# Dividing each pair's pooled rows by its sums of weights inside a copy, with chunks 1 to 3 reordered and short matmuls ahead of the program

## The chip, the cores and the metric

The kernel runs on one core of one Trainium2 chip. The metric is the device time of one execution in microseconds, as the median of 3 runs. One execution was also profiled, with every instruction and every DMA packet in time.

## The reference

Attention pooling of a recommendation model: 512 users, 200 behaviours each, 128 features.

```
h = relu(behavior @ W_b + (candidate @ W_c)[:, None, :] + fc1_b)      # 512 x 200 x 128
scores = h @ fc2_w + fc2_b                                            # 512 x 200
attn = softmax(scores, axis=-1)
user_interest = einsum('bse,bs->be', behavior, attn)                  # 512 x 128
x = concatenate([user_interest, candidate], axis=1)                   # 512 x 256
z = relu(x @ mlp1_w + mlp1_b)                                         # 512 x 256
logit = z @ mlp2_w + mlp2_b                                           # 512
```

All inputs are float32. The behaviours are 52 MB and are read twice, once as they are (`x`) and once transposed (`xt`).

## The kernel before

**Tiling.** A chunk is 16 users; there are 32 chunks, 0 to 31. A chunk's transposed data are four groups g0 to g3 of 800 columns. PE multiplies each group by `W_b` into one of three `z_ps` buffers of two banks; from chunk 2 on each group is six fp32r matmuls (L665, L666 and L669: high part by high weights, high part by low weights, low part by high weights), for which ACT makes the high part `xh` (L369) and DVE the low part `xl` (L500). A `z_ps` buffer is free again when its relu has been taken: g1 and g3 by ACT (L411, with the bias), g0 and g2 by DVE (L510, `biased_max`).

**Pairs.** Scores, softmax and pooling go by pairs of chunks. In the middle of each even chunk c from 4 on, after its group g1 (`PHASE_AT`), PE does: `transpose_sums` of an older pair (L733), `score` of chunks c-2 and c-1 (L682, 40 small fp32 matmuls), `weighted_sum` of chunks c-4 and c-3 into `u_ps` (L694, 56 small fp32 matmuls). Of fp32 matmuls every one leaves two load records and two matmul records in the trace, so the scores of a pair are 160 records, its weighted sums 224, and a group of six fp32r matmuls 12. DVE then takes the maxima of the scores (`softmax`, steps 0 to 6: step 0 is the transpose L521 and the last two make `exp_bias`, L540), ACT the exponentials with their row sums as an accumulated output (`exponents`, L376, `weight_sums`), and GpSimd spreads the weights by rows (`mask_weights`, L340). ACT copies the pooled sums of a pair from `u_ps` (`copy_pooled4`, L382), PE transposes them, ACT copies the result to `pooled_t` (L386).

**Start.** PE warms up with 9 matmuls of 128x128 by 128 (L799, unread output). Chunks 0 and 1 use plain fp32 products (L660). In `period`, phase 0, 1, 2 and 3 are chunks 0 to 3, and phase 4 is each later one but the last. In phase 1 and 3 ACT casts the first group of the next chunk before it takes the relu of g1. In phase 2 DVE does the whole softmax of chunks 0 and 1, and ACT their exponentials, before the last relu of chunk 2.

**Loops and queues.** `periods` writes chunks 0 to 3 out, and puts the rest in a loop over 4 chunks; PE's loop runs 7 times (chunks 4 to 31), and a straight tail follows. Each engine runs its list in order and waits on semaphores. All loads go through the queue that SP issues to, in a written order: per two chunks `xt` of c and c+1, then `x` of two older chunks, 1.6 MB each; SP waits for the buffer (four of each kind) before each.

**Tail.** The division by the sums of weights is done at the end in two parts (chunks 0 to 27, and 28 to 31). For each: `row_sums` (one matmul, L751), `inverses` on DVE (L549, L552), `spread_inverses` on PE (L757), `normalise` on DVE (L562), and then `mlp_pooled` (L776). The other operand of the MLP is `mlp_candidates` (L770), and `logits` (L783) ends each part. Chunks 30 and 31 have weighted sums of their own (`weighted_sum_alone`).

Of the kernel before, what the change touches and what calls it, by code (L numbers as in the profile page):

```python
# [11 lines left out]
P = 128  # L12
# [23 lines left out]
WARM_UP = 9  # L36
# [4 lines left out]
MASK_COLS = {"row_mask": 3 * ROWS, "fold": Q, "row_first": ROWS, "own_row": EACH, "same_row": P}  # L41
# [18 lines left out]
def attention_pooling_kernel(nc, behavior, behavior_t, cand_rest, weights_1, first, masks, later, out):  # L60
# [13 lines left out]
    with ExitStack() as ctx:  # L74
# [40 lines left out]
        row_mask, fold, row_first, own_row, same_row = (part_of(masks_sb, MASK_COLS, n) for n in MASK_COLS)  # L115
# [3 lines left out]
        pair_half = [slice(0, ROWS), slice(ROWS, 2 * ROWS)]  # L119
        row_mask = row_mask[:, ROWS:2 * ROWS]  # L120
# [11 lines left out]
        inv_sums = sb("inv_sums", [P, CHUNKS])  # L132

        inv_sel = xt[0][:, 0, 0:B].rearrange("p (c r) -> p c r", r=ROWS)
        pooled_n = xt[1][:, 0, 0:B]
# [14 lines left out]
        inverse_ps = [end_banks[0][1], end_banks[2][0]]  # L150
        mlp_ps = [end_banks[1], [s_ps[:, :], u_ps[:, :]]]
        logit_ps = [end_banks[2][1], inverse_ps[0]]
# [39 lines left out]
        mlp_step = [sem(f"mlp_step{i}") for i in range(2)]  # L192
        row_sums_done = sem("row_sums_done")
        inv_done = sem("inv_done")
# [158 lines left out]
        def _(act):  # L353
# [67 lines left out]
            def period(c, q, phase):  # L421
# [25 lines left out]
                biased_relu(c, q, 1, phase)  # L447
                for g in range(GROUPS):
                    next_half(g)

                for n in range(2):
                    exponents(c - 2 + n, n, pair_steps(c - 2) + 2 * (PAIR_STEPS - 1 + n), phase == 2)
                if phase > 2:
                    copy_pooled4(c - X_BUFS + 1, u_ps)
# [3 lines left out]
            copy_pooled_t(LAST - 4, u_ps[:, P:P + 2 * ROWS])  # L458
# [10 lines left out]
        def _(dve):  # L469
# [74 lines left out]
            def inverses(part, step):  # L544
                a, b = PART_CHUNKS[part]
                row_sums = inverse_ps[part]
                if step == 1:
                    dve.wait_ge(row_sums_done, part + 1)
                    op = nc.vector.reciprocal(inv_sums[:, a:b], row_sums[:, 0:b - a])  # L549
                if step == 2:  # L550
                    dve.wait_ge(mlp_step[part], 1)
                    op = nc.vector.tensor_tensor(  # L552
                        inv_sel[:, a:b, :], inv_sums[:, a:b].unsqueeze(2).to_broadcast([P, b - a, ROWS]),
                        row_first.unsqueeze(1).to_broadcast([P, b - a, ROWS]), ALU.mult)
                op.then_inc(mlp_step[part], 1)

            def normalise(part):
                a, b = PART_CHUNKS[part]
                inv = inverse_ps[part]
                dve.wait_ge(inv_done, part + 1)  # L560
                dve.wait_ge(pooled_t_copied, b + 2)
                nc.vector.tensor_tensor(pooled_n[:, a * ROWS:b * ROWS], inv[:, 0:(b - a) * ROWS],  # L562
                                        pooled_t[:, (a + 2) * ROWS:(b + 2) * ROWS], ALU.mult).then_inc(mlp_step[part], 1)
# [5 lines left out]
            def period(c, q, phase):  # L569
# [54 lines left out]
            inverses(0, 1)  # L624
            inverses(0, 2)
# [3 lines left out]
            normalise(0)  # L629
            inverses(1, 1)  # L630
            inverses(1, 2)
# [7 lines left out]
            normalise(1)  # L639
# [5 lines left out]
        def _(pe):  # L645
# [26 lines left out]
            def score(c, q, taken):  # L672
                pe.wait_ge(hidden_made, c * HALF + HALF)
                pe.wait_ge(relu_made, c * HALF + HALF)
                if taken is not None:

                    pe.wait_ge(softmax_step, taken)
# [30 lines left out]
            def weighted_sum(c, q):  # L708
                pe.wait_ge(x_loaded[q], loads(c, q))
                pe.wait_ge(masked, c + 1)  # L710
                if q % 2 == 0:

                    pe.wait_ge(pooled4_copied, c + 2)
                sum_tiles(c, q, u_ps, 0, WHOLE_TILES, GROUPS - 1).then_inc(pooled_done, 1)
# [31 lines left out]
            def row_sums(part):  # L746
                a, b = PART_CHUNKS[part]
                pe.wait_ge(weights_made, b)

                pe.wait_ge(relu_made, LAST * HALF + part + 1)  # L750
                nc.tensor.matmul(inverse_ps[part][:, 0:b - a], same_row, weight_sums[:, a:b],  # L751
                                 start=True, stop=True).then_inc(row_sums_done, 1)

            def spread_inverses(part):
# [152 lines left out]
```

## Time and profile before

| | |
|---|---|
| median of 3 runs | 267.79 us (267.74 to 267.81) |
| the profiled execution | 267.95 us |
| its span in the trace | 266.1 us (1.85 us lie around it) |
| PE busy | 254.9 us, 96% of the span |
| DVE, ACT, POOL busy | 205.4, 198.6, 28.9 us |
| DMA | 105.80 MB, busy to the ninth tenth or more in slices 2 to 37 of 40 |

Busy shares are means over stages. The chain that ended last is a path through the instructions, followed back from the last one. "Issue" is idle time of an engine for which no semaphore or transfer accounts in the profile. A row of the timeline is: start, length (us), engine, line, operation, output and inputs, count; in brackets the idle time before it and what ended it.

### The profile page before, as it was taken

The page shows a single profiled execution, that of the slowest core. Times are in us where ns is not written, and L with a number is a line of the kernel's source. Part 1 is how long each engine was busy: PE and PEld are TensorE (multiplying, and loading weights), DVE is VectorE, ACT ScalarE, POOL GpSimd, SP SyncE. Part 2 cuts the span into 40 slices and gives each one's busy share as a digit, 9 for nine tenths or more (in the row PEclk, how much of TensorE's full clock was granted, in tenths as well). Part 3 has the DMA queues.
Part 4 walks back from the last instruction along what each step waited for, and adds up shares of the span by engine and source line. Part 5 has one row for each costly group of instructions (what it writes and reads, how often), then busy time and mean ns, then how long its engine had stood idle before and what let it go on. Part 6 is the DMA issues. An engine that isn't in the chain of part 4 may idle for free.

```text
span 266.1 us, 10392 instructions
## 1 busy us (share of the span) xinstructions
PE 254.9 (96%) x3944; PEld 215.3 (81%) x3944; DVE 205.4 (77%) x316; ACT 198.6 (75%) x482; POOL 28.9 (11%) x39
## 2 busy tenths in 40 slices
PE   8989798979999999999999999999999999999795
PEld 7547587868888888888888888888888888888664
DVE  0458976977889796979798896979798997969221
ACT  2469685985969698896969696997887997957111
POOL 2000201102020110202020110202020201102100
PEclk9999799999999999999999999999999999999999
DMA  7999999999999999999999999999999999999700
GB/s 246 427 429 426 426 423 420 423 420 426 426 427 431 425 425 421 429 429 425 431 427 423 425 425 429 427 429 423 423 429 425 429 427 427 427 421 424 320 2 0
DMA packets 10684, 105.80 MB, mean 398 GB/s; under 512 B 1200, under 2 KB 1712, under 8 KB 2864
## 3 DMA queue, kind: packets, MB, share of 16 engines
q1 hardware_dynamic: 10384, 105.44, 94.3%
q10 hardware_dynamic: 288, 0.20, 0.2%
q8 instruction: 8, 0.13, 0.2%
q14 instruction: 4, 0.03, 0.0%
HBM read 105.63 MB, written 0.00 MB: 397 GB/s over the span
## 4 chain that ended last, share of the span: by engine, by line
PE 88%; DMA 4%; issue 3%; DVE 2%; SPq 1%; ACT 1%; DVEq 0%; ACTq 0%
PE z_ps L665 18%; PE s_ps L682 17%; PE z_ps L666 16%; PE z_ps L669 16%; PE u_ps L694 16%; DMA xt<-in_behavior_t 4%; PE z_ps L694 1%; PE z_ps L733 1%; PE z_ps L776 1%; SPq L263 1%; PE z_ps L770 1%; ACT hidden_rest L411 0%; DVE xl L500 0%; PE z_ps L757 0%; SPq L267 0%
## 5 line engine op out<-in xcount | busy, mean ns | idle before, releaser
L500 DVE TENSOR_TENSOR xl<-xt,xh 128x800 fp32r<-128x800 f32 x120 | 117.0, 1005 | 2.9 <-ACT xh L369 2.7
L369 ACT CAST xh<-xt 128x800 fp32r<-128x800 f32 x120 | 98.4, 888 | 10.7 <-DMA xt<-in_behavior_t 10.7
L665 PE MATMUL z_ps<-xh,w_hi 128*128 128x512 f32 x240 | 85.5, 356 | 2.4 <-ACT hidden_rest L411 1.2
L411 ACT ACTIVATE hidden_rest<-z_ps,bias 128x200 f32<-128x200 f32 x192 | 66.3, 428 | 28.0 <-PE z_ps L669 24.9
L666 PE MATMUL z_ps<-xh,w_lo 128*128 128x512 f32 x240 | 80.4, 349 | 0.0
L669 PE MATMUL z_ps<-xl,w_hi 128*128 128x512 f32 x240 | 64.2, 349 | 0.4 <-DVE xl L500 0.4
L665 PEld LDWEIGHTS z_ps<-xh,w_hi 128*128 128x128 f32 x240 | 45.5, 189 | 16.6 <-issue 4.4
L510 DVE TENSOR_TENSOR hidden_rest<-z_ps,neg_bias 128x800 f32<-128x800 f32 x48 | 47.2, 984 | 5.4 <-PE z_ps L669 3.0
L340 POOL TENSOR_TENSOR weights_by_row<-weights,masks_sb 128x400 f32<-128x400 f32 x31 | 27.0, 870 | 222.3 <-DVE xl L500 177.6
L666 PEld LDWEIGHTS z_ps<-xh,w_lo 128*128 128x128 f32 x240 | 45.5, 190 | 5.7
L694 PE MATMUL u_ps<-x,weights_by_row 128*32 128x128 f32 (+1 forms) x1680 | 44.8, 262 | 4.0 <-issue 4.0
L682 PE MATMUL s_ps<-hidden_rest,f_col 128*32 128x160 f32 (+4 forms) x960 | 46.5, 300 | 0.0
L694 PEld LDWEIGHTS u_ps<-x,weights_by_row 128*32 128x32 f32 x1680 | 42.0, 110 | 5.2 <-issue 4.6
L669 PEld LDWEIGHTS z_ps<-xl,w_hi 128*128 128x128 f32 x240 | 38.8, 190 | 1.2 <-DVE xl L500 0.7
L682 PEld LDWEIGHTS s_ps<-hidden_rest,f_col 128*32 128x32 f32 (+4 forms) x960 | 31.9, 90 | 4.1
L682 PE MATMUL s_ps<-hidden_first,f_col 128*32 128x160 f32 (+4 forms) x320 | 24.8, 301 | 0.0
L411 ACT ACTIVATE hidden_first<-z_ps,bias 128x200 f32<-128x200 f32 x64 | 22.6, 463 | 0.7 <-PE z_ps L660 0.7
L521 DVE STREAM_TRANSPOSE scores<-s_ps 128x320 f32<-128x320 f32 x16 | 8.3, 517 | 18.9 <-PE s_ps L682 10.0
L682 PEld LDWEIGHTS s_ps<-hidden_first,f_col 128*32 128x32 f32 (+4 forms) x320 | 14.2, 90 | 4.1
L376 ACT ACTIVATE weights<-scores,exp_bias 128x25 f32<-128x25 f32 x32 | 10.8, 338 | 7.7 <-DVE exp_bias L540 7.5
L510 DVE TENSOR_TENSOR hidden_first<-z_ps,neg_bias 128x800 f32<-128x800 f32 x16 | 15.7, 982 | 0.5 <-PE z_ps L669 0.5
L660 PE MATMUL z_ps<-xt,weights_sb 128*128 128x512 f32 (+1 forms) x32 | 12.1, 522 | 0.1
(70 smaller groups left out, 94.0 us busy)
## 6 DMA issues: line engine op xcount, KB each, us to landing
x<-in_behavior SPq DMA_DIRECT2D x31, 1600.0 KB, 20.4
xt<-in_behavior_t SPq DMA_DIRECT2D x30, 1600.0 KB, 18.2
xt<-in_behavior_t SPq DMA_DIRECT2D x4, 400.0 KB, 4.9
xt<-in_behavior_t SPq DMA_DIRECT2D x2, 800.0 KB, 7.7
x<-in_behavior SPq DMA_DIRECT2D x1, 832.0 KB, 13.3
x<-in_behavior SPq DMA_DIRECT2D x1, 768.0 KB, 14.7
later_sb<-in_later SPq DMA_DIRECT2D x1, 258.5 KB, 23.4
first_sb<-in_cand_rest SPq DMA_DIRECT2D x1, 192.0 KB, 5.7
```

Of the source, the lines that this page charges most:

```text
L340: nc.gpsimd.tensor_tensor(weights_by_row[buf][:, :, pair_half[buf]], weights[buf][:, :].unsqueeze(2).to_broadcast([P, TILES, ROWS]), row_m ...
L369: nc.scalar.copy(xh_of(q, g)[:, :], xt[q][:, g, :]).then_inc(xh_made, 1)
L376: nc.scalar.activation(weights[buf][:, :].rearrange("p (r t) -> p r t", t=RUN), score_runs(buf), ACT.Exp, bias=exp_bias[buf][:, :], accum_ ...
L411: op = nc.scalar.activation(hidden_of(q, g)[:, :, mine], z[:, :, mine], ACT.Relu, bias=bias[:, bass.ds(c * ROWS + g * EACH + b, 1)])
L500: nc.vector.tensor_tensor(xl[g][:, :], xt[q][:, g, :], xh_of(q, g)[:, :].bitcast(F32), ALU.subtract).then_inc(xl_made, 1)
L510: nc.vector.tensor_tensor(hidden_of(q, g)[:, :, :].rearrange("p t (b s) -> p t b s", s=PARTS), z, nb.to_broadcast([P, TILES, EACH, PARTS]) ...
L660: op = nc.tensor.matmul(z[:, a:b], w_b, xt[q][:, g, a:b], start=True, stop=True)
L665: nc.tensor.matmul(z[:, a:b], w_hi[:, :], xh_of(q, g)[:, a:b], start=True, stop=False)
L666: nc.tensor.matmul(z[:, a:b], w_lo[:, :], xh_of(q, g)[:, a:b], start=False, stop=False)
L669: op = nc.tensor.matmul(z[:, a:b], w_hi[:, :], xl[g][:, a:b], start=False, stop=True)
L682: op = nc.tensor.matmul(s_ps[g * Q:g * Q + rows, q % 2 * RUN * Q:(q % 2 + 1) * RUN * Q] .rearrange("p (t s) -> p t s", s=Q), f2_col[:, 0:r ...
L694: return nc.tensor.matmul(bank[g * Q:(g + 1) * Q, cols], weights_by_row[buf][:, t, :], x[q][:, t * E + cols.start:t * E + cols.stop], star ...
```

## The change

1. `row_sums(c, sums)` now makes the sums of weights of a pair, with two fp32 matmuls of 128x128 by one column. It stands ahead of the scores of every even chunk from 4 on, and twice in the tail. A DVE `reciprocal` per pair follows (`inverses`), ahead of the pair's softmax, and `copy_pooled4` multiplies by it on ACT. `spread_inverses`, `normalise` and the second half of `inverses` are gone.
2. ACT and DVE do chunks 1 to 3 in another order. In chunk 1 the relu of g1 comes before the casts of chunk 2. The softmax and the exponentials of chunks 0 and 1 move from the middle of chunk 2 to the end of chunk 3; only the transpose of the scores stays in chunk 2.
3. The warm-up is 6 matmuls and then 25 of 32 columns of weights by 8 columns, unread.
4. In the tail `mlp_pooled(0, m)` and `logits(0)` come earlier, the latter ahead of the weighted sums of chunk 31. The masks are 180 columns in place of 228.

```
-WARM_UP = 9
+WARM_UP = 6
+SHORT_WARM_UP = 25
-MASK_COLS = {"row_mask": 3 * ROWS, "fold": Q, "row_first": ROWS, "own_row": EACH, "same_row": P}
+MASK_COLS = {"row_mask": P + ROWS, "fold": Q, "own_row": EACH}
...
             def copy_pooled4(c, bank):
+                act.wait_ge(inv_made, c + 1)
                 act.wait_ge(pooled_done, c + 1)
-                nc.scalar.copy(pooled4[:, :], bank[:, 0:P]).then_inc(pooled4_copied, 2)
+                nc.scalar.mul(pooled4[:, :], bank[:, 0:P], inv_sums[:, :]).then_inc(pooled4_copied, 2)
...
+                if phase == 1:                       # ACT
+                    biased_relu(c, q, 1, phase)
+                    next_half(0)
+                    next_half(1)
+                    biased_relu(c, q, 3, phase)
+                    next_half(2)
+                    return
...
+                    if phase == 3:                   # ACT, end of chunk 3
+                        exponents(0, 0, pair_steps(0) + 2 * (PAIR_STEPS - 1), True)
+                        exponents(1, 1, pair_steps(0) + 2 * PAIR_STEPS, True)
...
+            def inverses(c, row_sums):
+                dve.wait_ge(row_sums_done, c + 2)
+                dve.wait_ge(pooled4_copied, c + 2)
+                nc.vector.reciprocal(inv_sums[:, :], row_sums).then_inc(inv_made, 2)
...
+                if phase == 1:                       # DVE
+                    biased_max(c, q, 2, phase)
+                    next_low(0)
+                    next_low(1)
+                    return
                 if q % 2 == 1:
-                    if phase > 1:
-                        low_half(c, q, 3)
+                    low_half(c, q, 3)
                     next_low(0)
                     biased_max(c, q, 2, phase)
                     next_low(1)
+                    if phase == 3:
+                        dve.wait_ge(shift_step, 3)
+                        for n in range(1, PAIR_STEPS):
+                            softmax(0, n, True)
                     return
                 low_half(c, q, 2)
                 low_half(c, q, 3)
                 if phase == 2:
                     shifts()
-                    dve.wait_ge(shift_step, 3)
-                for n in range(PAIR_STEPS):
-                    softmax(c - 2, n, phase == 2)
+                else:
+                    inverses(c - X_BUFS, row_sums_ps)
+                    for n in range(PAIR_STEPS):
+                        softmax(c - 2, n, False)
                 next_low(0)
                 next_low(1)
+                if phase == 2:
+                    softmax(0, 0, True)
...
+            def row_sums(c, sums):                   # PE
+                pe.wait_ge(weights_made, c + 2)
+                for n in range(2):
+                    op = nc.tensor.matmul(sums, pair_rows[n], weight_sums[:, bass.ds(c + n, 1)], start=n == 0,
+                                          stop=n == 1)
+                op.then_inc(row_sums_done, 2)
...
+            for n in range(SHORT_WARM_UP):
+                op = nc.tensor.matmul(z_ps[0][0:Q, 0:PARTS], ones[:, 0:Q], ones[:, 0:PARTS], start=True, stop=True)
...
                             transpose_sums(c - X_BUFS - 1, beside_z(q, g))
-                        score(c - 2, (q - 2) % X_BUFS, None if phase == 2 else pair_steps(c - 4) + 2)
-                        score(c - 1, (q - 1) % X_BUFS, None)
+                            row_sums(c - X_BUFS, row_sums_ps)
+                            pe.wait_ge(softmax_step, pair_steps(c - 4) + 2)
+                        score(c - 2, (q - 2) % X_BUFS)
+                        score(c - 1, (q - 1) % X_BUFS)
...
+            transpose_sums(LAST - 4, last_pair_ps[:, P:P + 2 * ROWS])
+            row_sums(LAST - 3, row_sums_ps)
+            pe.wait_ge(softmax_step, pair_steps(LAST - 3) + 2)
+            score(LAST - 1, (LAST - 1) % X_BUFS)
+            score(LAST, LAST % X_BUFS)
             weighted_sum(LAST - 3, (LAST - 3) % X_BUFS)
             weighted_sum(LAST - 2, (LAST - 2) % X_BUFS)
-            spread_inverses(0)
             for m in range(2):
                 mlp_candidates(0, m)
+            for m in range(2):
+                mlp_pooled(0, m)
             transpose_sums(LAST - 2, u_ps[:, P:P + 2 * ROWS])
+            pe.wait_ge(softmax_step, pair_steps(LAST - 1) + 2)
+            row_sums(LAST - 1, last_row_sums_ps)
+            weighted_sum_alone(LAST - 1)
             for m in range(2):
                 mlp_candidates(1, m)
-            row_sums(1)
-            weighted_sum_alone(LAST - 1)
-            mlp_pooled(0, 0)
-            mlp_pooled(0, 1)
-            spread_inverses(1)
+            logits(0)
             weighted_sum_alone(LAST)
-            logits(0)
             transpose_sums(LAST, last_pair_ps[:, P:P + 2 * ROWS])
-            mlp_pooled(1, 0)
-            mlp_pooled(1, 1)
+            for m in range(2):
+                mlp_pooled(1, m)
             logits(1)
```

## Rows read from the trace of the kernel before

**Rows 1.** Waits by engine: for what, us in total, times, longest.

```profile
DVE scores L521 <- PE s_ps L682: 10.0, 8, 2.2
```

**Rows 2.** Timeline of ACT and PE around the loads of chunks 29 and 31.

```profile
221.54 3.15 ACT L369 CAST xh<-xt 128x800 fp32r<-128x800 f32 x4 [2.17 <-DMA xt<-in_behavior_t]
236.91 3.15 ACT L369 CAST xh<-xt 128x800 fp32r<-128x800 f32 x4 [2.93 <-DMA xt<-in_behavior_t]
...
240.76 1.37 ACT L411 ACTIVATE hidden_rest<-z_ps,bias 128x200 f32<-128x200 f32 x4
...
242.41 0.39 PE L665 MATMUL z_ps<-xh,w_hi 128*128 128x512 f32 x1
```

**Rows 3.** Chain that ended last, steady stretch: start, us, what.

```profile
69.70 2.85 PE s_ps L682 x80
72.56 2.75 PE u_ps L694 x112
...
217.33 2.85 PE s_ps L682 x80
```

**Rows 4.** Timeline of PE, the three idle stretches put down to issue.

```profile
42.44 1.78 PE L694 MATMUL u_ps<-x,weights_by_row 128*32 128x128 f32 x60 [1.00 <-issue]
...
59.03 1.58 PE L694 MATMUL u_ps<-x,weights_by_row 128*32 128x128 f32 x56 [1.49 <-issue]
...
251.32 1.31 PE L694 MATMUL u_ps<-x,weights_by_row 128*32 128x32 f32 x42 [1.53 <-issue]
```

**Rows 5.** DMA queues at 40 to 42 us, then 46 to 47: packets, MB, share.

```profile
q8 instruction: 1, 0.02, 3.4%
...
q8 instruction: 1, 0.02, 6.9%
```

**Rows 6.** Timeline of PE in chunks 2 and 3, two of its waits.

```profile
18.94 0.47 PE L665 MATMUL z_ps<-xh,w_hi 128*128 128x512 f32 x1 [1.19 <-ACT hidden_rest L411]
...
29.81 0.62 PE L665 MATMUL z_ps<-xh,w_hi 128*128 128x512 f32 x1 [1.17 <-DVE hidden_rest L510]
```

**Rows 7.** Busy time by stretch: PE, PEld, DVE, ACT, POOL, granted clock, DMA share, GB/s.

```profile
26.60:30.03 3.43, 1.81 (x9) 1.15 (x8) 3.33 (x6) 2.83 (x9) 0.87 (x1) 1.00 1.00 422
30.00:33.40 3.40, 3.40 (x11) 2.91 (x11) 3.40 (x4) 1.35 (x5) 0.87 (x1) 0.51 1.00 420
```

**Rows 8.** Timeline of PE: a transpose in the loop, the row sums in the tail.

```profile
69.40 0.30 PE L733 MATMUL z_ps<-masks_sb,pooled 128*128 128x32 f32 x2
...
244.77 0.30 PE L751 MATMUL z_ps<-weight_sums,masks_sb 128*128 128x28 f32 x2
```

**Rows 9.** Timeline of DVE and ACT in chunks 2 and 3.

```profile
17.41 0.99 DVE L500 TENSOR_TENSOR xl<-xt,xh 128x800 fp32r<-128x800 f32 x1 [2.66 <-ACT xh L369]
...
25.22 0.25 DVE L527 TENSOR_REDUCE part_max<-scores 128x2 f32<-128x50 f32 x1
...
26.97 1.89 DVE L500 TENSOR_TENSOR xl<-xt,xh 128x800 fp32r<-128x800 f32 x2
...
27.10 0.33 ACT L376 ACTIVATE weights<-scores,exp_bias 128x25 f32<-128x25 f32 x1
```

**Rows 10.** Chain that ended last, in the tail.

```profile
245.29 2.85 PE s_ps L682 x80
...
249.79 1.53 issue
...
252.63 0.95 PE z_ps L757 x2
...
259.38 0.17 PE z_ps L757 x2
...
261.08 0.38 PE z_ps L783 x16
...
262.35 0.23 DVE xt L562
```

**Rows 11.** Timeline of PE, the warm-up.

```profile
1.00 4.21 PE L799 MATMUL z_ps<-ones 128*128 128x128 f32 x18 [1.00 <-POOL ones L323]
```

More of the change, by code:

```diff
@@ L114, in attention_pooling_kernel @@
         w_c, cand_t = (part_of(first_sb, FIRST_COLS, n) for n in FIRST_COLS)
-        row_mask, fold, row_first, own_row, same_row = (part_of(masks_sb, MASK_COLS, n) for n in MASK_COLS)
+        row_mask, fold, own_row = (part_of(masks_sb, MASK_COLS, n) for n in MASK_COLS)
         w_mlp, b_mlp, w_out, b_out = (part_of(later_sb, LATER_COLS, n) for n in LATER_COLS)
@@ L119, in attention_pooling_kernel @@
         pair_half = [slice(0, ROWS), slice(ROWS, 2 * ROWS)]
+        pair_rows = [row_mask[:, ROWS:], row_mask[:, 0:P]]
         row_mask = row_mask[:, ROWS:2 * ROWS]
@@ L149, in attention_pooling_kernel @@
         last_pair_ps = end_banks[0][0]
-        inverse_ps = [end_banks[0][1], end_banks[2][0]]
         mlp_ps = [end_banks[1], [s_ps[:, :], u_ps[:, :]]]
-        logit_ps = [end_banks[2][1], inverse_ps[0]]
+        logit_ps = [end_banks[2][1], end_banks[0][1]]
+        row_sums_ps = u_ps[:, P:P + 1]
+        last_row_sums_ps = s_ps[:, 2 * RUN * Q:2 * RUN * Q + 1]
         xt_piece = [sem(f"xt_piece{i}") for i in range(GROUPS - 1)]
@@ L191, in attention_pooling_kernel @@
         pooled_t_copied = sem("pooled_t_copied")
-        mlp_step = [sem(f"mlp_step{i}") for i in range(2)]
         row_sums_done = sem("row_sums_done")
-        inv_done = sem("inv_done")
+        inv_made = sem("inv_made")
         z_all_done = sem("z_all_done")
@@ L449, in period @@
                     next_half(g)
-                for n in range(2):
-                    exponents(c - 2 + n, n, pair_steps(c - 2) + 2 * (PAIR_STEPS - 1 + n), phase == 2)
                 if phase > 2:
+                    for n in range(2):
+                        exponents(c - 2 + n, n, pair_steps(c - 2) + 2 * (PAIR_STEPS - 1 + n), False)
                     copy_pooled4(c - X_BUFS + 1, u_ps)
@@ L628, in _ @@
             mask_last()
-            normalise(0)
-            inverses(1, 1)
-            inverses(1, 2)
+            inverses(LAST - 1, last_row_sums_ps)
             def add_out_bias(part):
@@ L638, in _ @@
             add_out_bias(0)
-            normalise(1)
             last_relu(0)
@@ L670, in products, with score @@
                 op.then_inc(z_done, 1)
-            def score(c, q, taken):
+            def score(c, q):
                 pe.wait_ge(hidden_made, c * HALF + HALF)
                 pe.wait_ge(relu_made, c * HALF + HALF)
-                if taken is not None:
-                    pe.wait_ge(softmax_step, taken)
                 for r in reversed(range(RUNS)):
@@ L744, in shift_sums @@
                 op.then_inc(shift_done, 1)
[L746 to L754, printed above, removed]
-                a, b = PART_CHUNKS[part]
-                pe.wait_ge(mlp_step[part], 2)
-                nc.tensor.matmul(inverse_ps[part][:, 0:(b - a) * ROWS], ones[:, :],
-                                 inv_sel[:, a:b, :].rearrange("p c r -> p (c r)"),
-                                 start=True, stop=True).then_inc(inv_done, 1)
+            def row_sums(c, sums):
+                pe.wait_ge(weights_made, c + 2)
+                for n in range(2):
+                    op = nc.tensor.matmul(sums, pair_rows[n], weight_sums[:, bass.ds(c + n, 1)], start=n == 0,
+                                          stop=n == 1)
+                op.then_inc(row_sums_done, 2)
             def mlp_candidates(part, m):
@@ L774, in mlp_pooled @@
                 a, b = (n * ROWS for n in PART_CHUNKS[part])
-                pe.wait_ge(mlp_step[part], 3)
-                nc.tensor.matmul(mlp_ps[part][m][:, 0:b - a], w_mlp[:, 0, m * P:(m + 1) * P], pooled_n[:, a:b],
-                                 start=False, stop=True).then_inc(z_all_done, 1)
+                pe.wait_ge(pooled_t_copied, PART_CHUNKS[part][1] + 2)
+                nc.tensor.matmul(mlp_ps[part][m][:, 0:b - a], w_mlp[:, 0, m * P:(m + 1) * P],
+                                 pooled_t[:, 2 * ROWS + a:2 * ROWS + b], start=False, stop=True).then_inc(z_all_done, 1)
             def logits(part):
@@ L863, in layout_constants @@
     zeros = np.zeros_like(row_mask)
-    each = [np.concatenate([zeros, row_mask, zeros], axis=1), p % Q == np.arange(Q)[None, :],
-            row_mask & (p % PARTS == 0), (p // Q % 2 == 0) & (p % Q // PARTS == np.arange(EACH)[None, :]),
-            p // PARTS == p.T // PARTS]
+    each = [np.concatenate(GROUPS * [zeros, row_mask] + [zeros], axis=1), p % Q == np.arange(Q)[None, :],
+            (p // Q % 2 == 0) & (p % Q // PARTS == np.arange(EACH)[None, :])]
     return [m.astype(np.float32) for m in each]
```

37 lines of the change are left out of this document (6 added, 31 removed).

## The prediction

> **What bounds the kernel now.** I read the table of busy times first, then the chain that ended last, the waits of PE, and last the timelines of ACT and of DMA. PE is busy for 96% of the span, and the chain runs through PE from chunk 2 on: PE sets the end. The DMA is close behind. It moves about 420 GB/s with a share of 1.00 even where PE stands half idle [rows 7], and the page shows no slice below nine tenths until the loads end. What the reader is to see in [rows 2]: ACT waits for the transposed data of chunk 29, and again of chunk 31, 15.37 us apart, and the wait has grown by 0.76 us. PE needs less for two chunks: from one pair's scores at 69.70 to those at 217.33 there are 10 pairs, 14.76 us each [rows 3]. So PE began far behind the loads and gains about 0.6 us on them with every pair. At chunk 31 it has nearly caught up: behind the four casts ACT ends the relu of chunk 30's g3 at 242.13 us, and PE's third group of chunk 31, which takes that relu's buffer, starts at 242.41 [rows 2]. Whatever PE gains before that place is worth 0.3 us at most; what it gains behind it counts in full, and so does what it loses anywhere.
>
> PE's idle time is in few places: three gaps with no semaphore behind them, 1.00, 1.49 and 1.53 us, each inside a run of small fp32 matmuls [rows 4], and some waits in chunks 2 and 3 [rows 6].
>
> **The gaps and the short matmuls.** A packet of queue q8 of the kind "instruction" starts between 40 and 42 us, ahead of the gap that ends at 42.44; another starts between 46 and 47, with products on PE, and no gap follows [rows 5]. I take q8 for PE's program. The two first gaps stand 492 records of the code apart (120 of weighted sums, 96 of eight groups, 4 of a transpose, 160 of scores, 112 of weighted sums) and two packets lie between, so a packet carries some 246 records. What PE had for the 246 records ahead of each gap, at 17.8 ns for a record of scores (2.85 us for 160) and 12.3 for one of sums (2.75 for 224) [rows 3], was 104 of sums and 142 of scores, 3.8 us; 112 and 134, 3.8; 140 and 106, 3.6. With the gap these are 4.8, 5.3 and 5.1. So a block takes about 5.1 us to come, and a block run faster than that costs the rest. The change adds 25 short matmuls and takes 3: 88 records more ahead of everything, and 8 more per pair for the row sums. The places move back by 96, 104 and 108 records (in the tail the row sums are two matmuls for one): from record 104, 112 and 140 of the weighted sums to 8, 8 and 32. The block ahead then holds the scores, 4 + 8 records and some 66 of products at 12 per 1.1 us (a pair's 14.76 less 5.90 for scores, sums and transpose, over eight groups): some 9 us. The next one holds 216 records of sums and 30 of products: 2.65 + 2.75 = 5.4 us, just enough. The third place's block would by the same count be asked for in the loop's first turn. I take all three as gone: -2.49 us before chunk 31 and -1.53 behind it; the bounds are 0 and -4.02.
>
> The Trainium skill (Runtime: NRT & Kernel Launch, Instruction fetch mechanics) has the program come in blocks of 16 KiB, 256 instructions, the next one fetched while the current one runs, and calls the cost of a boundary mostly hidden. The count of records agrees with the block's size. By "mostly hidden" the gaps would have another cause and the short matmuls would bring nothing.
>
> **Chunks 1 to 3.** Before, PE waits 1.19 us for the relu of chunk 1's g1 [rows 6], which stands on ACT behind a cast whose data land at 16.5. From 26.60 to 30.03 it is idle for 1.62 of 3.43 us, and then runs at half clock, 1.2 GHz, for 3.4 us [rows 7]: 1.7 us lost. Together 4.5 us. After, the relu comes first. DVE becomes the limit: from 17.41 [rows 9] it has 14 tensor operations ahead of the maxima of chunks 0 and 1, at 0.91 (two take 1.89 with 0.98 for the second), the shifts at 0.92 and the transpose at 0.5, and I allow 0.3 for casts that come late: 17.41 + 12.7 + 1.4 + 0.3 = 31.8 us. From the first maximum to the end of the second exponential are 2.3 us (25.22 to 27.10 + 0.33 and its accumulator's read, some 0.1 behind) [rows 9]: 34.1. PE's row sums in chunk 4 need these exponentials. By my walk, with groups at 1.1 us, PE is done with chunk 4's g1 and the transpose at 32.7, so it waits 1.4 us. Then row sums 0.44, scores 2.85, sums 2.75 [rows 3]: chunk 4's g2 starts at 40.2. Before it started at 44.22 [rows 4], of which 1.00 was the gap: the reordering gives 3.0 us, the first pair's row sums paid. The bounds are 1.2 (the first wait alone) and 4.5 (all of them).
>
> **Warm-up.** 18 records take 4.21 us [rows 11], so three matmuls are 1.4 us. 50 pairs of records of a short matmul: 24 ns each as in the logits (16 in 0.38 us) [rows 10] gives 1.2; by the columns moved, (32 + 8) of the (128 + 128) that take 0.234, it is 1.85. I take 1.7: +0.3 us.
>
> **Row sums.** The loop has no such matmul before. In the tail one (L751) stands between the last group and the transpose: from its start at 244.77 to the scores at 245.29 are 0.52 us [rows 8, 10]; without it, from 69.40 to 69.70, 0.30 [rows 3, 8]. So 0.22 each, nearly all of it the load of 128 columns of weights, and two are 0.44; the chain itself would say 0.14 each. 13 further pairs: +5.8 us (3.6 to 6.5), all on PE. DVE's reciprocal goes where DVE waits for the scores (8 of these waits are 10.0 us together) [rows 1], and ACT's multiplication for its copy is the same operation on the same data; both cost nothing under that wait, and a reciprocal's 0.2 or so per pair, as the small maxima next to it [rows 9], if the wait were gone. The new waits of `weighted_sum` and `copy_pooled4` for the inverse stand behind it in that slack.
>
> **To chunk 31** PE's account is -3.0 + 0.3 - 2.5 + 5.8 = +0.6 us: it comes 0.6 us later than before, so it is still PE and not the DMA that sets the pace (a pair takes 14.76 + 0.44 = 15.2 us against 15.37).
>
> **Tail.** Gone from the chain: the gap 1.53, `spread_inverses` 0.95 and 0.17, and on the last leg the `normalise`, 0.23 with some 0.05 of hand-over [rows 10]. Added: one matmul of row sums more in both places, 2 x 0.22, and `logits(0)`, 0.38, which was hidden behind ACT's last copy and now stands ahead of chunk 31's sums [rows 10]. `mlp_pooled(0, m)` moves, same cost. Sum: -2.9 + 0.8 = -2.1 us. The two relus of 448 columns lie under chunk 30's sums. The smaller masks save 25 KB, 0.06 us of DMA, which is not the limit.
>
> **Sum.** 266.1 + 0.6 - 2.1 = 264.6 us of span, with the 1.85 around it 266.4; the profiled execution stands 0.16 above the median, so 266.3 us.
>
> **Rivals.**
> - *The clock falls in chunk 4.* The wait of 1.4 us there, with 0.2 to 0.4 of small waits around it, is as much idle time as the 1.62 us after which it fell; it did not fall after gaps of 1.49 and 1.53 alone. Half clock for 3.4 us costs 1.7: 268.0, no change. A later rise of the clock at the start, since short matmuls are little work, has the same price.
> - *The DMA is the limit.* If row sums cost 0.14 each, or chunks 1 to 3 give 4.5, the account up to chunk 31 is below -0.3 and is held there by the loads: 266.1 - 0.3 - 2.1 + 1.7 = 265.4. More speed ahead of chunk 31 can't give less than that.
> - *The gaps stay* (the other side). They have another cause, or each moves with the sums: then 4.0 us of the forecast fail, 270.3 us, slower, since the row sums are paid with nothing. It decides from 2.0 us of gaps on. For it speaks that the packet at 46 to 47 has no gap behind it, so a fetch by itself stops nothing; against it, packets and gaps lie together, and a block's time comes out alike in all three. The Trainium skill's rule on that page, that the cost of a boundary is mostly hidden, is the same case.
>
> **How the numbers follow.** Forecast 0.49, the clock 0.20, the DMA 0.15, the gaps 0.16. Likeliest time 266.3. Down, the DMA's case is a floor at about 265.3, with 0.3 for the tail's terms 265.0; up, the clock's case with 0.4 of error is 268.4. What is left out above is the gaps' case. Within 0.2% (0.54 us, what a measurement of this kernel can tell) is 267.25 to 268.33: most of the clock's case and a little of the forecast and of half-gone gaps. Faster 0.63, same 0.22, slower 0.15.
>
> **What the profile will show.** No idle put down to issue in the weighted sums of chunks 4, 6 and the tail; packets of q8 elsewhere. Chunk 4's g2 near 40.2 us, with a wait of some 1.4 us for ACT's exponentials before it. Pairs of scores 15.2 us apart; near 14.8 would mean that row sums are nearly free, above 15.3 the DMA. ACT's wait for chunk 31 below 2.93 us. From the tail's scores to the end 18.5 us (now 20.8). The forecast is wrong if the clock drops after chunk 3, if a gap of over 1 us stays, or if a matmul by one column costs other than its load.

## The result and the profile after

The changed kernel takes 271.77 us (median of 4 runs, 269.78 to 272.80) against 267.8: 1.0138 times as long, 95% interval 1.0111 to 1.0164. It is slower by 4.0 us where 1.5 us less was forecast. The profiled execution, 269.78 us with a span of 268.0, is the fastest of the four; so two questions stand: where its own 1.8 us over the profiled execution before come from, and why most runs take some 2 us more still.

The page after: busy times and queue q8 (packets, MB, share).

```profile
PE 259.3 (97%) x4044; PEld 221.3 (83%) x4044; DVE 204.5 (76%) x326; ACT 200.3 (75%) x482; POOL 29.7 (11%) x39
...
q8 instruction: 9, 0.15, 0.2%
```

The waits of PE after: for what, us in total, times, longest.

```profile
PE u_ps L698 <- issue: 2.2, 1, 2.2
PE u_ps L755 <- ACT weights L377: 1.5, 1, 1.5
...
PE z_ps L672 <- issue: 0.5, 1, 0.5
```

The chain that ended last, after: start, us, what.

```profile
34.90 4.53 PE s_ps L686 x80
39.43 2.75 PE u_ps L698 x112
...
52.04 2.85 PE s_ps L686 x80
54.98 2.16 issue
...
62.92 0.50 issue
...
70.25 2.85 PE s_ps L686 x80
...
221.71 2.85 PE s_ps L686 x80
...
249.77 2.85 PE s_ps L686 x80
```

Read against those of before, the starts of the scores give the account of the profiled execution:

| start of scores | before | after | difference |
|---|---|---|---|
| chunk 8 | 69.70 [rows 3] | 70.25 | +0.55 |
| ten pairs on | 217.33 [rows 3] | 221.71 | +4.38 |
| tail | 245.29 [rows 10] | 249.77 | +4.48 |
| end of the span | 266.1 | 268.0 | +1.9 |

Ten pairs cost 3.83 us, 0.38 each (the pace is 15.15 us for 14.76); the tail gives 2.6 back. Both are near the forecast. The place that went wrong is ahead of chunk 8, where the new order and the gaps should have put PE 4.3 us ahead (3.0 + 2.5 - 0.3, less two pairs' row sums) and where it comes 0.55 late.

Two things stand there. The first is in chunk 4. PE's timeline after: start, us, line, operation, count, and the idle time before with what ended it.

```profile
32.50 0.30 PE L738 MATMUL z_ps<-masks_sb,pooled 128*128 128x32 f32 x2
34.30 0.60 PE L755 MATMUL u_ps<-weight_sums,masks_sb 128*128 x4 [1.50 <-ACT weights L377]
...
54.71 0.27 PE L698 MATMUL u_ps<-x,weights_by_row 128*32 128x128 f32 x1
57.15 2.95 PE L698 MATMUL u_ps<-x,weights_by_row 128*32 128x128 f32 x111 [2.16 <-issue]
...
63.42 0.29 PE L672 MATMUL z_ps<-xh,w_hi 128*128 128x288 f32 x1 [0.50 <-issue]
```

And the stretches around the scores of chunk 4: busy times of PE, PEld, DVE, ACT and POOL, granted clock, DMA share, GB/s.

```profile
35.60:39.00 3.40, 3.40 (x60) 2.26 (x56) 1.88 (x3) 2.60 (x6) 0.95 (x1) 0.50 1.02 429
39.10:42.50 3.40, 3.40 (x126) 3.14 (x115) 1.79 (x8) 1.35 (x3) 0.00 (x0) 1.00 1.00 419
```

PE waits 1.50 us for the exponentials of chunks 0 and 1, then the granted clock stands at 0.50, which is 1.2 GHz, for 3.4 us, and the 80 matmuls of scores take 4.53 us instead of 2.85: 1.7 us.

The second is the gaps. Before, they lay at records 104 and 112 of the weighted sums of chunks 4 and 6 [rows 4]. After, chunk 4 has none; in chunk 6 there are 2.16 us behind a single matmul of the weighted sums, and 0.50 more among the products at 63.42. Together 2.66 us for 2.49. By the count the first should stand at record 8; it stands at record 2. A packet of q8 goes ahead of each. The DMA queues after, from 54.70 to 54.85 us, show the first one, 2.4 us before the matmul at 57.15; the starts of packets given here and below are found by narrowing the window:

```profile
q8 instruction: 1, 0.02, 42.3%
```

### The profile page after: what moved, and what is told of

It reads as the page before. It is cut to its first block, busy times and chain, and to the rows that moved or that the text cites. A ratio compares the mean times of both kernels' runs of the same rounds, so it can differ in the third digit from the quotient of the medians.

```text
span 268.0 us, 10652 instructions
## 1 busy us (share of the span) xinstructions
PE 259.3 (97%) x4044; PEld 221.3 (83%) x4044; DVE 204.5 (76%) x326; ACT 200.3 (75%) x482; POOL 29.7 (11%) x39
## 4 chain that ended last, share of the span: by engine, by line
PE 90%; ACT 4%; DVE 3%; issue 2%; POOL 0%; DVEq 0%; ACTq 0%; POOLq 0%
PE s_ps L686 17%; PE z_ps L672 16%; PE u_ps L698 15%; PE z_ps L673 15%; PE z_ps L676 15%; PE z_ps L667 3%; PE u_ps L755 2%; DVE xl L513 2%; ACT xh L370 1%; PE z_ps L698 1%; PE z_ps L798 1%; ACT hidden_rest L414 1%; ACT hidden_first L414 1%; PE z_ps L738 1%; PE z_ps L801 1%
## 5 line engine op out<-in xcount | busy, mean ns | idle before, releaser
L672 PE MATMUL z_ps<-xh,w_hi 128*128 128x512 f32 x240 | 84.6, 352 | 0.5 <-issue 0.5
L673 PE MATMUL z_ps<-xh,w_lo 128*128 128x512 f32 x240 | 79.5, 347 | 0.0
L676 PE MATMUL z_ps<-xl,w_hi 128*128 128x512 f32 x240 | 63.3, 345 | 0.0
L341 POOL TENSOR_TENSOR weights_by_row<-weights,masks_sb 128x400 f32<-128x400 f32 x31 | 27.7, 896 | 226.1 <-DVE xl L513 186.0
L686 PE MATMUL s_ps<-hidden_rest,f_col 128*32 128x160 f32 (+4 forms) x960 | 48.2, 307 | 0.0
L698 PE MATMUL u_ps<-x,weights_by_row 128*32 128x128 f32 (+1 forms) x1680 | 44.2, 262 | 2.2 <-issue 2.2
L676 PEld LDWEIGHTS z_ps<-xl,w_hi 128*128 128x128 f32 x240 | 38.2, 188 | 0.2
L686 PEld LDWEIGHTS s_ps<-hidden_rest,f_col 128*32 128x32 f32 (+4 forms) x960 | 32.7, 93 | 4.7
L686 PE MATMUL s_ps<-hidden_first,f_col 128*32 128x160 f32 (+4 forms) x320 | 25.4, 306 | 0.0
```

The source lines that it names most:

```text
L341: nc.gpsimd.tensor_tensor(weights_by_row[buf][:, :, pair_half[buf]], weights[buf][:, :].unsqueeze(2).to_broadcast([P, TILES, ROWS]), row_m ...
L672: nc.tensor.matmul(z[:, a:b], w_hi[:, :], xh_of(q, g)[:, a:b], start=True, stop=False)
L673: nc.tensor.matmul(z[:, a:b], w_lo[:, :], xh_of(q, g)[:, a:b], start=False, stop=False)
L676: op = nc.tensor.matmul(z[:, a:b], w_hi[:, :], xl[g][:, a:b], start=False, stop=True)
L686: op = nc.tensor.matmul(s_ps[g * Q:g * Q + rows, q % 2 * RUN * Q:(q % 2 + 1) * RUN * Q] .rearrange("p (t s) -> p t s", s=Q), f2_col[:, 0:r ...
L698: return nc.tensor.matmul(bank[g * Q:(g + 1) * Q, cols], weights_by_row[buf][:, t, :], x[q][:, t * E + cols.start:t * E + cols.stop], star ...
```

## The experiments

Times are medians, with the range and the number of runs; ratios are to the kernel before on the same chip, with their 95% interval.

| kernel | us | ratio |
|---|---|---|
| before | 267.8 | 1 |
| shift_only | 269.59 (267.82 to 270.75, 10) | 1.0057 (1.0034 to 1.0081) |
| reorder_only | 267.74 (267.47 to 267.82, 10) | 0.9995 (0.9986 to 1.0005) |
| no_shift | 269.01 (268.82 to 269.31, 4) | 1.0043 (1.0026 to 1.0060) |
| no_division | 265.28 (264.59 to 266.55, 4) | 0.9904 (0.9866 to 0.9942) |
| rows_behind | 278.88 (278.87 to 278.90, 4) | 1.0408 (1.0391 to 1.0426) |
| short_47 | 275.15 (273.81 to 276.81, 4) | 1.0285 (1.0232 to 1.0338) |
| between_25 | 274.82 (272.17 to 275.60, 6) | 1.0277 (1.0256 to 1.0298) |
| between_9 | 269.32 (269.19 to 269.50, 4) | 1.0056 (1.0039 to 1.0072) |
| after_again | 269.21 (1) | |
| after_9_22 | 270.36 (269.76 to 273.54, 5) | 1.0088 (1.0069 to 1.0107) |
| reorder_shift | 265.97 (265.86 to 266.93, 6) | 0.9938 (0.9921 to 0.9955) |

**One part alone: the warm-up.** The kernel before, with the new warm-up and nothing else.

```diff
-WARM_UP = 9
+WARM_UP = 6
+SHORT_WARM_UP = 25
...
+            for n in range(SHORT_WARM_UP):
+                op = nc.tensor.matmul(z_ps[0][0:Q, 0:PARTS], ones[:, 0:Q], ones[:, 0:PARTS], start=True, stop=True)
```

> The kernel before with only the warm-up of the change (6 long and 25 short matmuls, 88 records more ahead of everything). Theory 1 (a gap of the program's fetch sits where a block boundary falls, and a block asked for late costs the rest): the gaps leave the places at 41.4, 57.5 and 249.8 us and stand some 88 records earlier, at the end of the scores; those before chunk 31 are worth at most 0.3 us because the loads hold PE there, the one in the tail 1.5: 266.0 us if it goes, 267.8 if it only moves. Rival (the gaps belong to the weighted sums and not to a boundary): all three stay where they are, 268.1 us with the longer warm-up.

Its chain, around chunk 6:

```profile
40.35 2.61 issue
...
59.30 0.27 PE u_ps L695 x12
59.57 2.34 issue
61.91 2.72 PE u_ps L695 x94
```

The places moved as counted, 88 records back: from records 104 and 112 of the weighted sums to 16 and 24 (8 and 12 matmul rows in the chain, each with its load), and the tail's gap is gone. But the two gaps grew to 2.61 and 2.34 us, where they had 1.00 and 1.49 [rows 4]; a fall of the clock follows the first. The kernel is 1.8 us slower. Its clock also rises later at the start, at 9.57 us for 6.14 before. So the places of the gaps are set by a count of instructions, as the prediction had it; their length is not what the prediction took it to be.

**Another part alone: the order of chunks 1 to 3.**

```diff
+                if phase == 1:
+                    biased_relu(c, q, 1, phase)
+                    next_half(0)
+                    next_half(1)
+                    biased_relu(c, q, 3, phase)
+                    next_half(2)
+                    return
...
+                    if phase == 3:
+                        exponents(0, 0, pair_steps(0) + 2 * (PAIR_STEPS - 1), True)
+                        exponents(1, 1, pair_steps(0) + 2 * PAIR_STEPS, True)
```

(with the matching edits on DVE)

> The kernel before with only the order of chunks 1 to 3 changed. Theory 1: PE does not wait in chunk 4, since no row sums stand there, only for the masks of the weights (0.3 to 0.8 us), the clock stays up, and chunk 4's g2 starts 4 us earlier than before; of these 0.3 us reach the end, since the loads hold PE at chunk 31: 267.5 us. Rival (the reordering by itself brings the clock down or makes DVE late for good): chunk 4 is not earlier and the time is 268 us or more.

The chain of reorder_only, and its group of casts:

```profile
32.74 2.85 PE s_ps L701 x80
...
36.95 1.37 issue
...
53.42 1.76 issue
...
245.14 2.85 PE s_ps L701 x80
```

```profile
L369 ACT CAST xh<-xt 128x800 fp32r<-128x800 f32 x120 | 98.2, 871 | 32.0 <-DMA xt<-in_behavior_t 31.9
```

The scores of chunk 4 start at 32.74, 4.5 us before the 37.22 of the kernel before: the upper bound of the forecast's term. The scores take 2.85 us, so the clock doesn't fall where nothing makes PE wait for the exponentials. And the time is the same, because the loads set the pace: ACT waits 31.9 us for them in all, and the tail starts at 245.14 for 245.29. That is the floor of the DMA, as read from [rows 2]: with PE at 14.7 us a pair, all that is won ahead of chunk 31 is worth 0.15 us.

**The change without its warm-up.**

```diff
-WARM_UP = 6
-SHORT_WARM_UP = 25
+WARM_UP = 9
+SHORT_WARM_UP = 0
```

> The changed kernel with the warm-up of before (9 long, no short matmuls). Theory 1: the gap of 2.2 us in chunk 6 and that of 0.5 in chunk 7 leave their places and come back 88 records later in the program, within the weighted sums, some 1.0 to 1.5 us each; the time stays within 1.5 us of the changed kernel's, 270 to 272, and its spread over runs may change. Rival: with the short matmuls gone the loss is gone too, and the time is 267 us or less.

The chain of no_shift:

```profile
33.81 0.60 PE u_ps L755 x4
34.41 4.53 PE s_ps L686 x80
...
55.73 1.70 issue
```

PE waits 1.5 us for the exponentials and the clock falls here too, so neither is the warm-up's. The four runs lie within 0.5 us of each other, and 2.8 us below the change; 270 to 272 was expected. The pairs are 15.13 apart.

**The change without the division by row.** no_division leaves the row sums, the reciprocals and the multiplication out of every pair and of the tail; its pooled rows are not divided by their sums of weights.

```diff
-                            row_sums(c - X_BUFS, row_sums_ps)
...
-                nc.scalar.mul(pooled4[:, :], bank[:, 0:P], inv_sums[:, :]).then_inc(pooled4_copied, 2)
+                nc.scalar.copy(pooled4[:, :], bank[:, 0:P]).then_inc(pooled4_copied, 2)
```

> The changed kernel without row sums, reciprocals and the multiplication by them (the pooled rows stay undivided; this part of the computation is left out). Theory 1 (row sums cost PE 0.42 us per pair, up to the pace of the loads): pairs at 14.7 us until PE has caught up with the loads, 15.35 after, no wait of 1.5 us in chunk 4; the tail's scores near 245.2, 17.5 us from there to the end: 264.5 us if no gap brings the clock down. Rival (the row sums are hidden behind something): pairs at 15.1 us all the same.

The chain of no_division:

```profile
35.41 2.85 PE s_ps L682 x80
38.48 2.60 issue
...
57.67 2.62 issue
...
72.09 2.85 PE s_ps L682 x80
...
189.62 2.85 PE s_ps L682 x80
...
246.19 2.99 PE s_ps L682 x80
```

From 72.09 to 189.62 there are eight pairs, 14.69 us each, against 15.15 with the division: 0.46 us a pair, all on PE. The loads' floor is not reached, against what was expected: PE keeps its 14.7 us a pair up to the tail, whose scores start 1.05 us later than in reorder_only. What stands ahead of it in this profile are two gaps, a fall of the clock, and a rise at the start at 10.63 us only. The gaps are 2.60 and 2.62 us with the places of shift_only. The clock falls behind a gap here: the granted clock is 0.5 from 41.35 for 3.4 us.

**The same sums behind the weighted sums.** PE's row sums stand behind the pair's weighted sums and DVE's reciprocal behind its softmax.

```diff
-                            row_sums(c - X_BUFS, row_sums_ps)
...
                             weighted_sum(c - 3, (q + 1) % X_BUFS)
+                            row_sums(c - X_BUFS, row_sums_ps)
...
-                    inverses(c - X_BUFS, row_sums_ps)
                     for n in range(PAIR_STEPS):
                         softmax(c - 2, n, False)
+                    inverses(c - X_BUFS, row_sums_ps)
```

> The changed kernel with the row sums of each pair behind its weighted sums on PE and their reciprocal behind the softmax on DVE. Theory 1: PE's wait of 1.5 us in chunk 4 shrinks to 0.5 (the masks), the granted clock does not fall in the scores of chunk 4 (2.85 us in place of 4.53), and 2.7 us of 3.2 are gained, 267 to 269 us. Rival (the clock falls for another reason, or the pace of the pairs is what costs): the scores of chunk 4 still take over 4 us and the time stays at 270 to 272.

The waits, and the chain of a pair:

```profile
DVE inv_sums L562 <- PE u_ps L754: 18.0, 15, 5.1
```

```profile
89.97 2.85 PE s_ps L686 x80
92.82 2.75 PE u_ps L698 x112
95.57 0.54 PE u_ps L754 x4
```

The wait of chunk 4 is gone, and the kernel is 11 us slower than before. DVE waits for PE's row sums in every pair, 18.0 us in all, and the `xl` that PE's products need stand behind that wait; the pairs are 15.54 us apart. The matmuls take 0.54 us at this place, not 0.42, which with the 14.69 of a pair without them makes 15.23. I put the other 0.3 down to the late `xl`, without a run of its own. Two gaps of 2.59 and 2.40 us stand ahead, and a fall of the clock goes with each.

**The same sums between scores and weighted sums**, in the bank of the scores: PE asks for the exponentials only where it needs them anyway. Once with the new warm-up, once with nine long matmuls and no short ones.

```diff
-                            row_sums(c - X_BUFS, row_sums_ps)
...
                         if phase > 2:
+                            row_sums(c - X_BUFS, last_row_sums_ps)
                             weighted_sum(c - 4, q)
```

> The changed kernel with the row sums of a pair between its scores and its weighted sums, in the scores' bank, and the reciprocal ahead of the softmax as it was. Theory 1 (PE's wait of 1.5 us in chunk 4 for the exponentials brings the clock down): the wait falls below 0.8 us, the clock stays up in the scores of chunk 4, the pairs stay at 15.1 to 15.2 us; 2.5 us below the changed kernel, 267.3 to 269.3, unless a fetch gap of over 2.4 us brings the clock down by itself. Rival (as in the run with the row sums behind the weighted sums, DVE is late for good): pairs at 15.4 us or more and 273 us or more.

> The same with the warm-up of before, so that block boundaries fall late in the weighted sums. Theory 1: gaps of 1.0 to 1.7 us in chunks 4 and 6, no fall of the clock anywhere, the tail's scores near 245.6 and 18.3 us from there to the end: 265.5 to 266.3 us, with a spread over runs below 0.5 us. Rival (the gaps are as large wherever the boundary falls): equal to the kernel with 25 short matmuls within 0.3 us.

The chain of between_9:

```profile
32.78 2.85 PE s_ps L686 x80
35.63 0.54 PE s_ps L754 x4
...
37.45 1.04 issue
...
54.12 1.04 issue
...
69.61 2.88 PE u_ps L698 x112
...
81.58 2.85 PE s_ps L686 x80
...
96.96 2.85 PE s_ps L686 x80
```

The scores of chunk 4 take 2.85 us in both, with no wait ahead of them: without the wait the clock stays up. In exchange every pair takes 15.36 us: the row sums 0.54, and the weighted sums behind them 2.88 for 2.75. With that, between_9 is level with no_shift, 269.32 to 269.01, and not at the 265.5 to 266.3 that was expected. between_25, the same but for the warm-up, takes 5.5 us more, as its rival had it; in its profile the clock rises at 12.44 us for 4.25, and PE reaches the scores of chunk 4 at 36.30 for 32.78.

**More short matmuls.** The change with 47 for 25, so that a boundary falls into the scores.

```diff
-SHORT_WARM_UP = 25
+SHORT_WARM_UP = 47
```

> The changed kernel with 47 short matmuls in place of 25 (88 records more), so that the block boundaries of chunks 4 and 6 fall in the middle of the scores. The step of the prediction (a block is asked for at the entry of the one before it and comes 5 us later): no gap in chunk 6 at all. Theory 2 (a block whose entry lies among the products is asked for late, near the scores, wherever the boundary is): a gap of over 2 us in the middle of the scores of chunk 6, and the time no better than 269.5 us. The clock falls in chunk 4 by both.

Its timeline at the start:

```profile
3.86 5.18 PE L801 MATMUL z_ps<-ones 128*32 128x8 f32 x94
8.97 3.04 PE L667 MATMUL z_ps<-xt,weights_sb 128*128 128x512 f32 x4
```

The gap at the start of chunk 6's weighted sums is gone, and another of 1.78 us is at 62.62, in their last quarter, at the next boundary of the program; none falls into the scores. So neither expectation of the gaps came true. The second was not put to the test: with these 88 records more the block ahead is entered in the weighted sums of chunk 4, and no longer among products. The 94 records take 5.18 us, and the first products 3.04 for four; the clock rises at 14.04 us. It is 3.4 us slower than the change.

**What the spread is made of.** The change once more, and the change with nine long matmuls and 22 short ones, which leaves every place in the program where it was.

```diff
-WARM_UP = 6
-SHORT_WARM_UP = 25
+WARM_UP = 9
+SHORT_WARM_UP = 22
```

> The changed kernel once more, for a second profile of it; the first one was of the fastest of four executions, 269.78 us, where the granted clock rose at 4.9 us. Theory 3 (six long matmuls and short ones are too little work, and when the clock rises is left to chance): this execution takes 271 to 273 us, and its clock rises at 8 us or later. Rival (the spread is that of the fetch gaps): the clock rises near 5 us again and the gap of chunk 6 or the one of chunk 4 is longer by the difference.

> The changed kernel with 9 long and 22 short matmuls: the program stands at the same places, 88 records behind that of before, but the warm-up is as strong as before. Theory 3: the clock rises at 4 to 6.5 us, and the spread over runs shrinks; 269.5 to 270.5 us, 1.5 to 2 below the changed kernel. Rival (the place of the gaps makes the spread): median 271 to 272 and a spread of 3 us as before.

The first products in PE's timeline, after:

```profile
5.95 1.61 PE L667 MATMUL z_ps<-xt,weights_sb 128*128 128x512 f32 x4
```

The same in after_9_22:

```profile
7.59 3.04 PE L667 MATMUL z_ps<-xt,weights_sb 128*128 128x512 f32 x4
```

The same in the kernel before:

```profile
5.00 2.08 PE L660 MATMUL z_ps<-xt,weights_sb 128*128 128x512 f32 x4
```

And the chain of after_9_22:

```profile
39.23 4.27 PE s_ps L686 x80
...
59.05 1.88 issue
```

Four records of the first products take 1.61 us after, 3.04 in after_9_22 and 2.08 before. The clock records of the traces have the step to 2.4 GHz at 4.16 us in after_again (span 267.4), at 4.89 after (268.0) and at 13.18 in after_9_22 (271.8). The view of stretches gives 1.00 for the time before that step, so the durations of the matmuls have to be read. From 4.16 to 13.18 us of waiting for the clock the span grows by 4.4 us, some half of it, as it must when PE works at half speed. What follows the start is nearly alike in all three: 1.5 us of wait, slow scores, a gap of 1.9 to 2.2. So these three profiles differ by little else than the start. That the other runs of one program differ by it too is likely, and not shown: they left no trace. The other profiles belong to the same picture: without short matmuls the step lies at 4.25 to 6.14 us (between_9, no_shift, reorder_only, before), with them at 4.16 to 14.04, and in six of nine at 9.31 or later (rows_behind, shift_only, no_division, between_25, after_9_22, short_47). after_again was the run of the change that came early where a late one was to be caught; after_9_22 was to rule a late one out and shows one: its profiled execution is the slowest of its five, 273.54, and the others lie at 269.8 to 270.4. Nine long matmuls are no guarantee with short ones behind them.

**A version out of what held.** The order of chunks 1 to 3 and 22 short matmuls behind nine long ones; the division and the order of the tail stay as before.

```diff
 (reorder_only)
+SHORT_WARM_UP = 22
```

> The kernel before with the new order of chunks 1 to 3, its own warm-up and 22 short matmuls behind it; the division stays at the end. With the new order alone PE ran into the pace of the loads and 1.45 us of gap were left in the tail. Theory: the larger gaps of chunks 4 and 6 (2.6 each) and a fall of the clock after them are still paid by the room before the loads, the tail's scores start at 245.2 us, and the tail's gap is gone: 264.5 us of span, 266.3 us. Rival (the room is too small, 5.2 + 1.7 us of losses): the tail's scores start later than 246 us and the time is 267.5 or more.

Its chain in the tail:

```profile
244.90 2.85 PE s_ps L702 x80
247.75 2.75 PE u_ps L714 x112
```

It is faster than both kernels: 265.97 us, 0.9938 of before (0.9921 to 0.9955). The tail's scores start at 244.90, at the loads' floor, although its profile has a gap of 2.43 us at 52.66, the only one of the two that were expected, and a fall of the clock behind it: PE has the room for both. The tail is 19.1 us for 20.8 before, since its gap of 1.53 is gone. Between it and after_9_22, which has the same warm-up, stand the division and the tail's new order: 4.4 us. How late the clock rises is in that number too: at 5.03 us in the one profile, at 13.18 in the other.

## Why the prediction was wrong

The forecast of 266.3 us stood on steps that I take in its order.

- **"I take all three as gone" failed.** After, the gaps of chunk 4 and of the tail are gone, that of chunk 6 is longer, and one of 0.50 us is new; in shift_only only the tail's is gone. The count of places was right within some six records: the gaps moved to the start of the weighted sums. What failed is "a block takes about 5.1 us to come", counted from PE's entry into the block ahead. By the forecast that block is entered early, among products, and the next would be there in time. The packets say otherwise. In shift_only the packet of q8 starts at 40.57 and the gap ends at 42.96; after, 54.76 and 57.15; the time from the packet to PE's next matmul is 2.4 us in both. In the kernel before it is 40.02 and 42.44. But where the entry lies among the products some 7 us ahead of the scores, the packet starts no sooner: 3.3 us behind the start of the scores in shift_only, 2.7 after, 2.8 in the kernel before, whose block ahead is entered in the scores. So the short matmuls bring the boundary forward and don't bring the packet forward with it. In chunk 6 this holds in every profile with short matmuls but short_47. In chunk 4 the packet comes sooner in five of them (after: 33.35, ahead of the scores), and no gap follows there. From a known entry, the end of a gap, the next packet takes 3.8 us (42.44 to 46.22 before) and the block 6.2, not 5.1; over the profiles it is 3.4 to 4.1 us to the packet and 2.3 to 2.7 from there. The term: -4.02 forecast, -1.36 measured (0.17 worse ahead of chunk 8, 1.53 better in the tail).

  Why a block entered among products is asked for late stays open. The gaps of 2.16 us and more have packets that start within 0.3 us of PE's stop (40.57 for 40.35 in shift_only), and the boundary lies some 3 us behind the start of the scores there; so whether such a block is asked for by the scores or only when PE stands at the boundary can't be told apart.

  For the tail the prediction's reason holds, by the order of the packets: the sixth one, which comes ahead of the tail's gap at 248.75 us before, comes at 68 to 163 us in the nine profiles with short matmuls and at 248.6 to 250.5 in the four without. It is fetched in the loop, where nothing waits for it (94.54 after, the loop's second turn, not its first). But the short matmuls were not needed for that gap: in no_shift and between_9 the packet comes at 250.4 and 250.5, and their tails have no gap either.

- **The rule of the rival.** The Trainium skill (Runtime: NRT & Kernel Launch, Instruction fetch mechanics) calls the cost of a boundary mostly hidden. Of the boundaries inside products that is what the runs show, but for 0.50 us. Inside the weighted sums they cost 1.0 to 2.6 us in most cases, but 0.25 us or nothing in chunk 4 of seven profiles; those that fall into the scores cost nothing.

- **"The clock falls in chunk 4" happened.** The wait was sized right, 1.5 us for 1.4. The fall's price too: 1.7. It was held for the less likely case (0.20), since the clock did not fall behind 1.5 us alone [rows 4]. Five profiles show the wait and the fall together (after, after_again, after_9_22, no_shift, short_47), and between_25, between_9 and reorder_only neither. A gap in a run of small matmuls is another matter: 2.16 us went by without a fall, and with five of seven gaps from 2.34 to 2.62 us one came, in or behind the gap. That the small waits around this one make the difference was argued, and is not shown.

- **"A later rise of the clock at the start [...] has the same price" came on top.** The warm-up was sized +0.3 us, by the time that its matmuls take. The short ones take 2.16 us after, for the 1.7 forecast, and the first products start 0.95 us later than before (5.95 for 5.00); part of this came back in the profiled execution, since its clock rose at 4.89 us for 6.14 before. The runs show what it costs in the clock: seven of the eight kernels with short matmuls spread over 1.1 to 3.8 us (rows_behind over 0.03, in four runs), the three experiments without them over 0.3 to 0.5, and the kernel before over 1.4 in the worst set, of 11 runs. From between_9 to between_25 it is 5.5 us, from no_shift to the change 2.8; these pairs differ by the whole warm-up, the places and lengths of the gaps included. The 2.0 us by which the median lies above the profiled execution would be a rise some 4 us later than its 4.89, by the half of each us found above; that is an estimate, since those runs left no trace.

- **The new order** was worth what it was sized: chunk 4's g2 at 42.18 us, which is 40.5 without the clock's 1.7, for 40.2.

- **The row sums** took 0.42 us of the forecast 0.44 on PE, and the pace was 15.15 for 15.2. No part of them was hidden: without them it is 14.69. Ten pairs cost 3.83 for 4.4.

- **The tail** took 18.2 us from its scores, for 18.5.

- **The DMA's floor** was read rightly from [rows 2]: reorder_only and reorder_shift reach the tail's scores at 245.14 and 244.90, and in reorder_only ACT waits for loads 31.9 us in all. The change itself never came near it: ACT waits 0.8 us.

The sum again, with what was measured: 266.4 forecast for the profiled execution, +1.7 for the clock, +2.66 for the gaps, -0.7 for the row sums (13 pairs of 0.383 for 0.44), makes 270.1; it took 269.78. The 2.0 us from there to the median of 271.77 are put down to a later rise of the clock, by the estimate above and not by a trace. Each of these terms was on the prediction's list. The error was to hold the clock, the gaps and the start as rivals of which one may come: they came together, and the chances of 0.16 and 0.20 hid 4 us and more.

## What to carry to other kernels

Count the rivals that don't exclude each other as terms of the sum before you give them chances. Before work is moved into the loop, ask which engine sets the pace there: here 0.42 us a pair on PE, 14 times, was paid in full, while the same division at the end cost some 1.4 us once (`spread_inverses` and `normalise`) [rows 10]. And look at the start before you move a program's boundaries: what a shift by small matmuls saves at the end it may lose in the clock at the beginning.

## What was unexpected of the hardware

- The same program reached 2.4 GHz at 4.16 and 4.89 us, and with three long matmuls more and three short ones fewer at 13.18. Between the first and the last lie 4.4 us of span. The Trainium skill (TensorE: Matmul & The Clock Gate, Part 1: The HAM clock gate) says that the moment varies from run to run by 500 ns to either side. The two traces of one program, 0.73 us apart, agree; the 9 us to after_9_22 are outside it.
- A gap for code ended 2.3 to 2.7 us behind the start of its packet in all 13 profiles, whatever the place of the gap; its length is set by when the packet starts.
- A matmul by one column, 0.21 us at the place of the change, takes 0.27 behind the scores or the weighted sums (0.54 for two).
